# Perceiver layer with a top-2 mixture of experts: the down projection of all full blocks in three fp32r products, three blocks behind gate and up

## The reference, cut to what matters

```python
scores = jnp.einsum('btd,de->bte', x, router_w)
probs = jax.nn.softmax(scores, axis=-1)
routing_weights, routing_idx = jax.lax.top_k(probs, TOP_K)
...
gate = jnp.einsum('bted,edf->btef', dispatched, gate_proj)
up = jnp.einsum('bted,edf->btef', dispatched, up_proj)
acts = jax.nn.silu(gate) * up
expert_out = jnp.einsum('btef,efd->bted', acts, down_proj)
return jnp.einsum('bted,bte->btd', expert_out, expert_w)
```

## Time and profile before

| | |
|---|---|
| median of 3 runs | 1846.14 us |
| profiled execution, its own time | 1845.26 us |
| its span | 1843.2 us |
| mean granted TensorE clock over the span | 0.909 |
| busy: PE, PEld, DVE, ACT, POOL | 1516.0, 1175.5, 1300.7, 778.1, 97.1 us |
| stage of the experts, first gate and up to the end | 1233.6 to 1843.2 us |

### The profile page before, as it was taken

One profiled execution on the slowest core, in us unless ns is written; L12 is line 12 of the kernel. 1 busy time (PEld: TensorE's weight loads), 2 busy tenths in 40 slices (PEclk: granted clock), 3 DMA queues, 4 the chain that ended last, 5 costly groups with the idle time before them and its releaser, 6 DMA issues. The chain is left out here.

```text
span 1843.2 us, 22920 instructions
## 1 busy us (share of the span) xinstructions
PE 1516.0 (82%) x7393; PEld 1175.5 (64%) x7393; DVE 1300.7 (71%) x2782; ACT 778.1 (42%) x1433; POOL 97.1 (5%) x261
## 2 busy tenths in 40 slices
PE   6999999999799999519400059759999999999997
PEld 3888888888677767403100058647777777777774
DVE  4376557655425786999999936457787777777777
ACT  2333433333344544301000042236667676676763
POOL 0000000000000000003111100040000000000004
PEclk9999999999899999859755559869999999999999
DMA  3210111010132531440100042255425515235104
GB/s 121 81 35 17 34 34 34 17 34 17 50 89 54 96 51 49 94 147 36 46 0 0 0 120 69 79 206 188 173 80 203 191 41 211 96 139 188 36 18 143
DMA packets 134205, 152.99 MB, mean 83 GB/s; under 512 B 64096, under 2 KB 84960, under 8 KB 134112
## 3 DMA queue, kind: packets, MB, share of 16 engines
q1 hardware_dynamic: 128384, 137.68, 24.4%
q0 software_dynamic: 2560, 8.39, 1.4%
q10 hardware_dynamic: 3168, 5.77, 0.9%
HBM read 250.25 MB, written 31.33 MB: 153 GB/s over the span
## 5 line engine op out<-in xcount | busy, mean ns | idle before, releaser
L1786 DVE TENSOR_TENSOR gl<-w_gu,gh 128x2048 fp32r<-128x2048 f32 x138 | 290.3, 2104 | 6.7 <-ACT gh L1712 6.6
L1712 ACT CAST gh<-w_gu 128x2048 fp32r<-128x2048 f32 x138 | 243.5, 1766 | 38.7 <-PEq L1413 19.2
L1634 PE MATMUL bank<-gh,xh 128*128 128x512 f32 (+1 forms) x552 | 218.5, 396 | 1.7 <-DVE xl L1777 1.4
L1636 PE MATMUL bank<-gh,xl 128*128 128x512 f32 (+1 forms) x552 | 206.3, 374 | 0.0
L1635 PE MATMUL bank<-gl,xh 128*128 128x512 f32 (+1 forms) x552 | 205.9, 373 | 0.0
L1229 PE MATMUL bank<-o_v,xnT 128*128 128x64 f32 x256 | 36.1, 310 | 178.1 <-DMA o_v<-scratch_v_rows 178.1
L1229 PEld LDWEIGHTS bank<-o_v,xnT 128*128 128x128 f32 x256 | 35.8, 227 | 178.9 <-DMA o_v<-scratch_v_rows 178.9
L539 DVE COPY probT<-bank 128x512 f32<-128x512 f32 x64 | 41.1, 683 | 127.9 <-PE bank L421 127.9
L1828 DVE TENSOR_TENSOR hid<-silu,bank 128x256 f32<-128x256 f32 x138 | 54.7, 396 | 107.7 <-ACT silu L1739 104.3
L1064 ACT ACTIVATE r_root<-r_nm 128x8 f32<-128x8 f32 x32 | 6.7, 209 | 275.4 <-DVE r_nm L1142 275.4
L1634 PEld LDWEIGHTS bank<-gh,xh 128*128 128x128 f32 x552 | 104.3, 189 | 19.4 <-DVE xl L1777 2.4
(11 more groups left out here) (306 smaller groups left out, 3486.4 us busy)
## 6 DMA issues: line engine op xcount, KB each, us to landing
w_gu<-in_gate_proj SPq DMA_DIRECT2D x46, 1024.0 KB
w_gu<-in_up_proj SPq DMA_DIRECT2D x46, 1024.0 KB
w_d<-in_down_proj SPq DMA_DIRECT2D x46, 1024.0 KB
w_gu<-in_gate_proj SPq DMA_DIRECT2D x23, 768.0 KB
w_gu<-in_up_proj SPq DMA_DIRECT2D x23, 768.0 KB
w_d<-in_down_proj SPq DMA_DIRECT2D x23, 768.0 KB
ctx_raw<-in_ctxT SPq DMA_DIRECT2D x32, 385.5 KB, 3.7
scratch_x_slots<-r_outw SPq DMA_DIRECT2D x1, 5888.0 KB, 19.6
```

The lines of the kernel that those rows point to most:

```text
L1634: pe.matmul(bank, xh[s % 2][:, k, :], hi, start=(k == 0), stop=False)
L1636: mm = pe.matmul(bank, xl[s % 2][:, k, :], hi, start=False, stop=(k == KC - 1))
L1712: nc.scalar.copy(gh[n % RING][:, :, :, 0:bw].rearrange("p k a f -> p (k a) f"), w_gu[:, :, :, b * BLK:b * BLK + bw].rearrange("p k a f -> ...
L1786: nc.vector.tensor_tensor(gl[n % RING][:, :, :, 0:bw].rearrange("p k a f -> p (k a) f"), w_gu[:, :, :, b * BLK:b * BLK + bw].rearrange("p ...
```

## The change

The down projections of all five full blocks (b = 0 to 4) are made in three fp32r products; block 5 keeps one fp32 chunk. The down projection runs LAG = 3 steps behind gate and up instead of 2. gh and gl become rings of 3, hh, hl and dh rings of 3, dl a ring of 2, hT one chunk. On ScalarE gh(n+3) always stands directly behind silu(n), and take_hidden(n-1) and dh(n-1) follow. On VectorE gl(n+2) stands behind hid(n), then dl(n-2), then hl(n-1), each for full blocks alone. The first two sums of gathered rows stand one step later. `full(n)` is b < 5, and `fulls(n)` the number of full blocks ahead of n.

```diff
-RING = 4
+RING = 3
+LAG = 3
...
-        hh, hl = sb("hh", [P, BLK // P, P], F32R), sb("hl", [P, BLK // P, P], F32R)
-        hT = [hh, sb("hT", [P, BLK // P, P])]
-        dh, dl = sb("dh", [P, BLK // P, C], F32R), sb("dl", [P, BLK // P, C], F32R)
+        hh, hl = ([sb(f"{name}{i}", [P, BLK // P, P], F32R) for i in range(LAG)] for name in ("hh", "hl"))
+        hT = sb("hT", [P, P])
+        dh, dl = ([sb(f"{name}{i}", [P, BLK // P, C], F32R) for i in range(k)] for name, k in (("dh", LAG), ("dl", 2)))
...
+        FULL = F // BLK
+        full = lambda n: n % NB < FULL
+        fulls = lambda n: n // NB * FULL + min(n % NB, FULL)
...
-                        if n % 2 == 0:
-                            pe.wait_ge(hl_done, n // 2)
+                        pe.wait_ge(hl_done, fulls(n - 1))
...
-                    if b % 2 == 0:
-                        pe.wait_ge(d_in[b // 2], 16 * (s + 1))
...
-                    if b % 2 == 0:
-                        pe.wait_ge(dl_done, n // 2 + 1)
-                        pe.wait_ge(hl_done, n // 2 + 1)
-                        for c in cs:
-                            pe.matmul(bank, hh[:, c, :], dh[:, c, :], start=(b == 0 and c == 0), stop=False)
-                            pe.matmul(bank, hh[:, c, :], dl[:, c, :], start=False, stop=False)
-                            mm = pe.matmul(bank, hl[:, c, :], dh[:, c, :], start=False, stop=False)
+                    if full(n):
+                        pe.wait_ge(dl_done, fulls(n) + 1)
+                        pe.wait_ge(hl_done, fulls(n) + 1)
+                        for c in range(BLK // P):
+                            w_hi, w_lo = dh[n % LAG][:, c, :], dl[n % 2][:, c, :]
+                            pe.matmul(bank, hh[n % LAG][:, c, :], w_hi, start=(b == 0 and c == 0), stop=False)
+                            pe.matmul(bank, hh[n % LAG][:, c, :], w_lo, start=False, stop=False)
+                            mm = pe.matmul(bank, hl[n % LAG][:, c, :], w_hi, start=False, stop=False)
                     else:
-                        for c in cs:
-                            mm = pe.matmul(bank, hT[1][:, c, :], w_d[:, b * (BLK // P) + c, :], start=False,
-                                           stop=(b == NB - 1 and c == cs[-1]))
+                        pe.wait_ge(d_in[b // 2], 16 * (s + 1))
+                        mm = pe.matmul(bank, hT[:, :], w_d[:, FULL * (BLK // P), :], start=False, stop=True)
                     mm.then_inc(d_done, 1)
...
-                for n in range(STEPS + 2):
+                for n in range(STEPS + LAG):
                     if n < STEPS:
                         gate_up(n)
-                    if n >= 2:
-                        down(n - 2)
+                    if n >= LAG:
+                        down(n - LAG)
...
-                    if n >= 2:
-                        act.wait_ge(d_done, n - 1)
-                    nc.scalar.copy(hT[n % 2][:, 0:bw // P, :].rearrange("p c n -> p (c n)"),
-                                   ps[H_BANK + n % 2][:, 0:bw]).then_inc(hT_done, 1)
+                    if n >= LAG:
+                        act.wait_ge(d_done, n - LAG + 1)
+                    into = hh[n % LAG][:, :, :].rearrange("p c n -> p (c n)") if full(n) else hT[:, :]
+                    nc.scalar.copy(into, ps[H_BANK + n % 2][:, 0:bw]).then_inc(hT_done, 1)
...
                     act.wait_ge(d_in[b // 2], 16 * (s + 1))
-                    if n >= 2:
-                        act.wait_ge(d_done, n - 1)
-                    nc.scalar.copy(dh[:, :, :], w_d[:, b * (BLK // P):(b + 1) * (BLK // P), :]).then_inc(dh_done, 1)
+                    nc.scalar.copy(dh[n % LAG][:, :, :], w_d[:, b * (BLK // P):(b + 1) * (BLK // P), :]).then_inc(dh_done, 1)
...
-                for n in range(STEPS + 2):
+                for n in range(STEPS + LAG):
                     if n < STEPS:
...
-                    if n % 2 == 0 and n + 3 < STEPS:
+                    if n + 3 < STEPS:
                         split_gate_up(n + 3)
                     if 1 <= n <= STEPS:
                         take_hidden(n - 1)
-                    if n % 2 == 0 and n < STEPS:
-                        split_down(n)
-                    if n >= 2 and (n - 2) % NB == NB - 1:
-                        store_y((n - 2) // NB)
-                    if n % 2 and n + 3 < STEPS:
-                        split_gate_up(n + 3)
+                        if full(n - 1):
+                            split_down(n - 1)
+                    if n >= LAG and (n - LAG) % NB == NB - 1:
+                        store_y((n - LAG) // NB)
...
-                    dve.wait_ge(dh_done, n // 2 + 1)
-                    nc.vector.tensor_tensor(dl[:, :, :], w_d[:, b * (BLK // P):(b + 1) * (BLK // P), :], dh[:, :, :].bitcast(F32),
-                                            ALU.subtract).then_inc(dl_done, 1)
+                    dve.wait_ge(dh_done, fulls(n) + 1)
+                    if n >= 2:
+                        dve.wait_ge(d_done, n - 1)
+                    nc.vector.tensor_tensor(dl[n % 2][:, :, :], w_d[:, b * (BLK // P):(b + 1) * (BLK // P), :],
+                                            dh[n % LAG][:, :, :].bitcast(F32), ALU.subtract).then_inc(dl_done, 1)
+
+                def split_hidden(n):
                     dve.wait_ge(hT_done, n + 1)
-                    nc.vector.tensor_tensor(hl[:, :, :].rearrange("p c n -> p (c n)"), ps[H_BANK][:, 0:BLK],
-                                            hh[:, :, :].rearrange("p c n -> p (c n)").bitcast(F32), ALU.subtract).then_inc(hl_done, 1)
+                    nc.vector.tensor_tensor(hl[n % LAG][:, :, :].rearrange("p c n -> p (c n)"), ps[H_BANK + n % 2][:, 0:BLK],
+                                            hh[n % LAG][:, :, :].rearrange("p c n -> p (c n)").bitcast(F32),
+                                            ALU.subtract).then_inc(hl_done, 1)
...
-                    if n % 2 and n < STEPS:
-                        split_down(n - 1)
                     if 0 < n < STEPS - 2:
                         split_gate_up(n + 2)
+                    if n >= 2 and full(n - 2):
+                        split_down(n - 2)
+                    if n >= 1 and full(n - 1):
+                        split_hidden(n - 1)
...
-                    if STEPS - 3 <= n < STEPS:
-                        gather_sum(n - STEPS + 3)
-                for t in range(3, NT):
+                    if STEPS - 2 <= n < STEPS:
+                        gather_sum(n - STEPS + 2)
+                for t in range(2, NT):
                     gather_sum(t)
```

More of the change, by code:

```diff
@@ L1651, in down @@
                     pe.wait_ge(hT_done, n + 1)
-                    if b % 2 == 0:
-                        pe.wait_ge(d_in[b // 2], 16 * (s + 1))
                     if b == 0 and s >= 2:
                         pe.wait_ge(y_ready, s - 1)
-                    cs = range(width(b) // P)
                     bank = ps[Y_BANK + s % 2]
-                    if b % 2 == 0:
-                        pe.wait_ge(dl_done, n // 2 + 1)
-                        pe.wait_ge(hl_done, n // 2 + 1)
-                        for c in cs:
-                            pe.matmul(bank, hh[:, c, :], dh[:, c, :], start=(b == 0 and c == 0), stop=False)
-                            pe.matmul(bank, hh[:, c, :], dl[:, c, :], start=False, stop=False)
-                            mm = pe.matmul(bank, hl[:, c, :], dh[:, c, :], start=False, stop=False)
-                    else:
-                        for c in cs:
-                            mm = pe.matmul(bank, hT[1][:, c, :], w_d[:, b * (BLK // P) + c, :], start=False,
-                                           stop=(b == NB - 1 and c == cs[-1]))
+                    if full(n):
[6 more added lines that the diff above has]
+                            mm = pe.matmul(bank, hl[n % LAG][:, c, :], w_hi, start=False, stop=False)
+                    else:
+                        pe.wait_ge(d_in[b // 2], 16 * (s + 1))
+                        mm = pe.matmul(bank, hT[:, :], w_d[:, FULL * (BLK // P), :], start=False, stop=True)
                     mm.then_inc(d_done, 1)
                 pick_first()
-                for n in range(STEPS + 2):
+                for n in range(STEPS + LAG):
                     if n < STEPS:
                         gate_up(n)
-                    if n >= 2:
-                        down(n - 2)
+                    if n >= LAG:
+                        down(n - LAG)
                     if 1 <= n <= STEPS:
```

## The result

The changed kernel takes **1939.26 us** (median of 4 runs, 1933.48 to 1941.57) against 1846.81 us of the kernel before beside it (4 runs): a ratio of 1.0498, 95% interval 1.0479 to 1.0517. The forecast was 1937 us.

A forecast was written before the change was run, and what follows sets the result against it. TensorE was taken to bound the expert stage, busy 25.20 of 25.20 us a tile. 1845.3 + 34.8 (dl waits, products included) + 3.0 (later y) + 52.5 (loads) + 1.0 (start) gave 1937 us; bounds 1905 to 1961, range 1880 to 1962.

The forecast's parts named there:

- Part 1: TensorE's down projections: blocks 1 and 3 go from 1.72 to 1.37 us each, 0.70 us less a tile.
- Part 2: TensorE waits for dl, made behind gl on VectorE: period 26.79 instead of 25.21 us, +34.8 us over 22 tiles.
- Part 4: Gate and up loads issued later on SyncE at seven changes of expert: 7.5 us each, +52.5 us.
- Part 3: A tile's y is stored one step later because the down projection runs three behind: +3.0 us.
- start: First steps of the stage, with only gate and up on TensorE: gl may be late, +1 us (-1 to +3).
- S: Moment when TensorE leaves gate and up of block n; dl(n-2) was forecast to end at S + 4.37 us.
- about as much then: Placement work on VectorE in the fifth tile: stalls TensorE 2.73 us before, and about the same after the change.
- a wait of 1 to 2 us there is covered: ScalarE's load point in tiles of the same expert: such a wait costs nothing, since gl has until step 4.
- loads hidden: Rival on SyncE's loads: they stay hidden, leaving only the dl waits and the later y, 1884 us; chance 0.08.
- TensorE still the bound: Rival: dl and the loads are in time, so the kernel gets faster, 1833 us; chance 0.06.
- The clock in every tile: Rival: the 1.06 us wait lowers TensorE's clock in 15 more tiles, 1.7 us each, 1962 us; chance 0.05.

The follow-up runs named there:

- the kernel with its three orders mended: Changed kernel with dl ahead of gl and xl ahead of hl on VectorE, and next-tile loads ahead of the last down load on SyncE: 1831.98 us.
- Loads early: Changed kernel with SyncE issuing a tile's last down load behind the next tile's first two gate and up loads: 1882.41 us.

## Why the prediction was right

The stage from the first gate and up to the end grew from 609.6 to 700.8 us, by 91.2; the forecast's terms sum to 91.3. Ahead of it 5.1 us came on top, which I take for spread (first gate and up at 1238.67 instead of 1233.57; in the other kernels' traces it lies between 1231.4 and 1238.1, with the same code ahead of it). The stage in pieces, with turn_x as the mark of a tile:

| | forecast, us | measured, us |
|---|---|---|
| 21 periods, parts 1 and 2 | 21 x 1.58 = 33.2 | 21 x 1.66 = 34.9 |
| seven loads and the placement, part 4 | 52.5 | 85.8 - 34.9 = 50.9 |
| ends of the stage: one more period, part 3, start | 1.6 + 3.0 + 1.0 = 5.6 | 6.1 |
| behind the last y | 0 | -0.8 |

(85.8 is the distance from the first to the last turn_x, 623.4 against 537.6 us.)

- **Part 1**, 0.70 us a tile: 0.58 in the kernel with its three orders mended, of which some 0.08 is still a wait for xl. The changed kernel never shows it.
- **Part 2**, period 26.79: 26.86 to 26.89. The down projections of the trace above follow each other by 4.46, 4.43, 4.41, 4.64 and 4.45 us, and the next by 4.47; the forecast's steps were 4.48, 4.45, 4.42, 4.51, 4.42 and 4.51. The waits forecast at 1.06 and 0.70 are 1.03 and 0.80. The one that is off starts 0.26 us behind dl's end (1553.63 + 1.22) where 0.14 was put; dl itself is there 4.38 us after S (4.37 forecast). Why the answer took 0.26 there and 0.10 at 1537.17 I can't tell. That dl's place is the cause, and not the products, is shown from both sides: 1.90 us a tile less with dl first, 1.9 more in the kernel before with dl and hl late.
- **Part 3**, 3.0 us: not isolated, but with the start's 1.0 it is what the ends of the stage grew by beyond one period. Measured so it is 6.1 - 1.7 = 4.5 us here and 3.8 in the kernel with its three orders mended, where 4.0 stood.
- **Part 4**, 7.5 us per change: a fresh tile takes 34.6 to 35.2 us, 7.7 to 8.4 over a plain one. From issue to landing 8.86 (8.8 forecast), gh wait 7.60 (7.7), delay 6.65 less the plain tile's 0.87, so 5.8 (5.8). The clock was sized too small: 3.4 us at 0.50 and 4.0 at 0.85 are 2.3 us lost, not 1.7; TensorE had stood 6.65 us where the earlier trace rows had 2.73. Two things made up for it. The placement cost 5.5 us before (30.75 against 25.21) and only some 2.9 over a fresh tile now (37.79 - 26.87 - 8.0); "about as much then" was wrong. Of the 5.5 some 1.2 were the load of that tile, as the kernel before with early loads shows (29.59). And the loads of before had already cost 2.7 us in three more tiles, which "a wait of 1 to 2 us there is covered" denied.

Where the rest of the placement's saving comes from the windows behind its stands show (clock in the third column from the right):

```profile
1373.88 0.50 PE L1638 MATMUL bank<-gh,xh 128*128 128x512 f32 x1 [1.77 <-DVE gl L1782]
1378.08 0.47 PE L1663 MATMUL bank<-dh,hh 128*128 128x512 f32 x1 [1.14 <-DVE dl L1792]
```

```profile
1373.90:1377.90 4.00, 3.03 (x12) 2.15 (x12) 4.00 (x5) 0.98 (x3) 0.00 (x0) 1.00 0.81 307
```

TensorE stands twice, for gl and for dl, but its clock stays 1.00, where the kernel before has 0.57 behind 2.73 us. The forecast put the placement at its old price, with that loss of clock in it. It is not that the placement hides behind a load: the stand for that tile's load ends at 1355.06, 10 us before the placement's work begins.

So the mechanism held in both of its causes, but that the sum came within 0.1 us of the stage was partly luck: errors of +1.7, -1.6, +0.5 and -0.8 cancelled, and within part 4 a price per change that was 0.5 us too low, seven times, met the two savings just named.

Of the rivals, *loads hidden* is what "Loads early" makes, 1882 where 1884 stood. *TensorE still the bound* was 1833; it takes three edits of order, and then it is 1832. The agreement is partly chance, since the early loads bring some 5 us that this rival had not counted. *The clock in every tile* did not come: after 0.87 us the plain tile shows 1.00. The Trainium skill (Perfetto Trace Analysis, Identifying the Most-Contended Engine) has the engine with the highest occupancy optimized first, and would judge TensorE's headroom by the share of its peak that it reaches and by the busy share of its weight loads, which the forecast left out. In the trace that share is 19.32 of 25.20 us in the earlier trace rows, 77%, beside 78% for VectorE, which decides nothing here. That TensorE was the bound the runs show: eased, and with the queues in order, the kernel gains 0.7%, 0.3 of it by early loads alone. The same relief brings a loss of 5% when VectorE's and SyncE's queues answer too late.

The misses lay in the expectations of the experiments, and mostly in one step: to take one instruction as the only one for which a place waits (dl without hl, dl without xl), or a count of projections for a count of steps.

## What to carry to other kernels

Sum the work of an engine, but then put each result's time beside the moment at which the bounding engine reaches it: VectorE had 22.3 us of work in a tile of 24.5 and was late four times. A longer lag helps only the operands whose making is not moved along with it. And look at what a queue waits for ahead of a load: one wait for the slowest consumer, put in front of the next tile's first load, cost 8 us at each change of weights, and moving it behind them cost nothing that shows.

## What the hardware showed

- A load of two pieces of 1 MiB took 8.9 us from issue to landing, although the queues moved 397 GB/s in 5.4 us of them: 2.1 MB at that rate are 5.3 us. About 2.4 us pass ahead of the full rate, in which most of x and y (0.26 MB each) moves, and at least 0.5 us between the last byte and gh. The Trainium skill (DMA: Bandwidth & Descriptors, Bandwidth) has 341 GB/s for 1 MB, by which I estimated 6.2 us for this load. Its figures are for loads that GpSimd issues and count the time in which the DMA engines are busy, so they stand beside the trace's 397 GB/s, which are faster, and not beside the 8.9 us; for the wait of gh the trace's time decides.
- The second of two loads in one queue did not slow the first: with the second issued 9.1 us later (1439.31) the first landed after 8.9 us, and with it 1.2 us behind too.
- After a stand of 6.65 us TensorE's granted clock was 0.50 for at least 3.4 us; after 0.87 and 0.64 us, in each plain tile, it stayed 1.00. The length of one stand did not settle it: at the placement the clock stayed 1.00 for 4 us after 1.77 us in the changed kernel, but it was 0.57 over 4 us after 1.76 us in "Loads early":

```profile
1355.30:1359.30 4.00, 4.00 (x11) 3.17 (x12) 4.00 (x5) 0.07 (x1) 0.00 (x0) 0.57 0.59 136
```
